# Two-layer transformer block: how VectorE finishes the mLSTM heads, and where it reads the causal mask

## What is computed

```
log_D = log_fg + ig                      (lower triangle, -inf above it)
D = exp(log_D - max_log_D)
C = (q @ k.T / sqrt(32)) * D
normalizer = max(|C.sum(-1)|, exp(-max_log_D))
h = (C / (normalizer + EPS)) @ v
hn = (h - h.mean(-1)) * rsqrt(h.var(-1) + EPS) * ln_scale        (over the 32 channels of a head)
x = x + hn
```

## Time and profile before

| | us |
|---|---|
| median of 3 runs | 1285.64 |
| lowest, highest | 1282.01, 1287.48 |
| the profiled execution, its own time | 1286.82 |
| span of its trace | 1285.0 |
| mean granted TensorE clock | 0.927 of full |
| PE busy | 1093.1 |
| DVE busy | 854.9 |
| ACT busy | 523.9 |
| POOL busy | 417.1 |

### The profile page before, as it was taken

How to read it: one execution, slowest core, us unless ns; L and a number is a source line. 1 busy time by engine, 2 the same in 40 slices (tenths; PEclk the granted TensorE clock), 3 DMA queues, 4 the chain that set the end, 5 groups by cost and what they waited for, 6 DMA issues and landing times. The chain is left out here.

```text
span 1285.0 us, 21982 instructions
## 1 busy us (share of the span) xinstructions
PE 1093.1 (85%) x6180; PEld 826.6 (64%) x6198; DVE 854.9 (67%) x1561; ACT 523.9 (41%) x1092; POOL 417.1 (32%) x327
## 2 busy tenths in 40 slices
PE   6999799788887759887859996999999999999842
PEld 6989666434443428777847764777777777777630
DVE  3547449878875628888756895767677676766415
ACT  1332152366674258677524242433333333333210
POOL 0000001111110201666733001456566556655420
PEclk8999899999999788888768999999999999999975
DMA  7323500100000486534063312878789898777539
GB/s 276 135 98 155 204 25 1 17 1 0 0 1 1 154 287 224 199 145 181 1 248 145 71 56 82 238 182 231 187 235 233 203 234 224 200 191 176 81 63 378
DMA packets 100284, 185.19 MB, mean 144 GB/s; under 512 B 13737, under 2 KB 32425, under 8 KB 100240
## 3 DMA queue, kind: packets, MB, share of 16 engines
q1 hardware_dynamic: 79856, 141.33, 32.6%
q0 software_dynamic: 18080, 38.85, 15.6%
q10 hardware_dynamic: 2304, 4.46, 0.9%
HBM read 138.50 MB, written 50.86 MB: 147 GB/s over the span
## 5 line engine op out<-in xcount | busy, mean ns | idle before, releaser
L2235 POOL DMA_INDIRECT y_d<-tail,x_ox x80 | 169.0, 2112 | 135.6 <-ACT tail L2400 110.1
L1536 POOL DMA_INDIRECT x_g<-r_d,x_ix x82 | 87.2, 1063 | 138.6 <-issue 115.6
L2293 PE MATMUL x_h<-x_w_hi,x_t_hi 128*128 x320 | 128.1, 400 | 2.2 <-DVE x_t_lo L2416 2.2
L2294 PE MATMUL x_h<-x_w_lo,x_t_hi 128*128 x320 | 127.7, 399 | 0.0
L2295 PE MATMUL x_h<-x_w_hi,x_t_lo 128*128 x320 | 127.7, 399 | 0.0
L210 POOL TENSOR_TENSOR ln_rstd<-ln_ve,powers 128x2 f32<-128x2 f32 (+1 forms) x40 | 26.2, 655 | 265.5 <-DVE ln_ve L204 265.5
L2416 DVE TENSOR_TENSOR x_w_lo<-w,x_w_hi (+1 forms) x64 | 109.6, 1753 | 2.6 <-ACT x_w_hi L2374 2.6
L2365 ACT ACTIVATE x_gs<-x_h 128x256 f32<-128x256 f32 x80 | 30.7, 385 | 187.5 <-PE x_h L2295 172.4
L2416 DVE TENSOR_TENSOR x_t_lo<-x_xb,x_t_hi 128x512 fp32r<-128x512 f32 x80 | 55.3, 692 | 43.0 <-ACT x_t_hi L2360 42.8
L1268 ACT ACTIVATE h_d<-h_negm,h_g 128x256 f32<-128x256 f32 x128 | 63.7, 498 | 28.6 <-DVE h_negm L1440 26.8
L2312 PE MATMUL x_o<-x_w_hi,x_avt_hi 128*128 x160 | 72.0, 450 | 1.5 <-issue 1.1
(11 more groups left out here) (371 smaller groups left out, 2671.8 us busy)
## 6 DMA issues: line engine op xcount, KB each, us to landing
w<-in_L_ffn_w SPq DMA_DIRECT2D x32, 1024.0 KB, 8.6
h_negm<-negm_d SPq DMA_DIRECT2D x16, 1024.0 KB, 7.1
w<-in_L_ffn_w SPq DMA_DIRECT2D x32, 512.0 KB, 10.0
raw<-in_L_ffn_w SPq DMA_DIRECT2D x3, 2816.0 KB, 16.8
x_res<-in_x SPq DMA_DIRECT2D x8, 512.0 KB, 4.9
ctx_in<-in_ctx SPq DMA_DIRECT2D x8, 512.0 KB, 3.5
...
```

The source lines that it names most:

```text
L1536: nc.gpsimd.indirect_dma_start(out=xg[q][s][:], out_offset=None, in_=r_d, in_offset=bass.IndirectOffsetOnAxis(ap=ix[q][:, s:s + 1], axis=0 ...
L2235: nc.gpsimd.indirect_dma_start(out=y_d[s], out_offset=bass.IndirectOffsetOnAxis(ap=ox[q][:, s:s + 1], axis=0), in_=eo[q][s][:], in_offset= ...
L2293: nc.tensor.matmul(hbank[s][:], hi[:, k, :], w13p[0][:, at, k, :], start=k == 0, stop=False)
L2294: nc.tensor.matmul(hbank[s][:], hi[:, k, :], w13p[1][:, at, k, :], start=False, stop=False)
```

## The change

- The squares are taken of the raw rows, not of the divided ones: variance = nrm * nrm * (sum of raw squares) / 32 + EPS. The 1024-element division on DVE is gone; POOL multiplies the raw rows by ln_scale (one instruction of 1024 elements in place of two of 512), and the two factors var^-0.5 and nrm are multiplied on POOL (a new instruction on 32 columns) before they meet the rows. One buffer `hb` is left of two.
- DVE's finishing steps are three pieces: `norms_of` behind group 1 (3 instructions), `variance` behind group 2 (the sum alone), and the new `scale` behind group 3 (3 instructions on 32 columns, the last of which releases POOL's power).
- ACT's `square` moves from behind group 1 to behind group 0, and no longer waits for DVE.
- `later`, a copy of the causal mask, is made once in PSUM (DVE), and `mask` reads it there. The two banks of `tg` become one, and EPS is added where the floor is copied.
- `weigh` becomes two instructions of 768 elements, two heads each; `c_ready` and `qk_ps` count halves, and the scores of the first two heads of a group wait only for the first half of the weigh before.
- `soft_log(0)` on ACT stands one batch of gates earlier.
- The last batch's steps in `experts` are changed in the same way; `tail_divide` is gone, and its small steps stand in `tail_variance`.

The first product now waits for the raw rows alone; the power still waits for DVE, and one small product stands between the power and the big one. The diff, cut to its core (line numbers of the functions behind it shift by 2 to 15):

```diff
     hr = [sbuf(st, "h_raw", [P, CB, NH, W])[:], tail.raw]
-    hb = [sbuf(st, "h_b", [P, CB, NH, DH])[:], tail.h]
-    sq, nrm, var, rs = tail.sq, tail.nrm, tail.var, tail.rs
+    hb = tail.h
+    sq, nrm, nrm2, var, rs = tail.sq, tail.nrm, tail.nrm2, tail.var, tail.rs
 
 
     qk = psum(st, "h_qk", [P, HG, 512])
     pvb = [psum(st, f"h_pv{i}", [P, CB, HG + WIDE - 1, W]) for i in range(2)]
     gbank = [t[:].rearrange("p c h w -> p (c h w)")[0:2 * NH, 0:S] for t in pvb]
-    tg = [psum(st, f"d_tg{j}", [P, CB, BH]) for j in range(2)]
+    tg = psum(st, "d_tg", [P, 2, CB, BH])
+    later = psum(st, "h_later", [P, P])
 
     w_sum, a_step, g_step, xn_ready, xt_ps, xt_sb, g_ps, g_sb = (
...
@@ -1200,22 +1202,24 @@
 
         def finish(b, u):
 
-            h = hb[u]
-            flat = h.rearrange("p c h e -> p c (h e)")
-            pool.wait_ge(sq_ready, b + 1)
-            for c in range(CB):
-                steps.did(nc.gpsimd.tensor_tensor(flat[:, c], flat[:, c], lns[:], ALU.mult))
+            pool.wait_ge(h_sb, NG * b + NG)
+            nc.gpsimd.tensor_tensor(hb, hr[u][:, :, :, 0:DH],
+                                    lns[:].rearrange("p (h e) -> p h e", e=DH).unsqueeze(1).to_broadcast([P, CB, NH, DH]),
+                                    ALU.mult).then_inc(scaled, 1)
             pool.wait_ge(var_ready, OPEN + b + 1)
             nc.gpsimd.tensor_tensor(rs.rearrange("p c h -> p (c h)"), var.rearrange("p c h -> p (c h)"),
                                     powers[:, 0:1].to_broadcast([P, CB * NH]), ALU.pow).then_inc(rs_ready, 1)
             pool.wait_ge(rs_ready, OPEN + b + 1)
-            steps.settle()
-            steps.then(nc.gpsimd.tensor_tensor(h, h, rs.unsqueeze(3).to_broadcast([P, CB, NH, DH]), ALU.mult))
-            nc.gpsimd.tensor_tensor(x[:, ds(CB * b, CB), :], x[:, ds(CB * b, CB), :], flat, ALU.add).then_inc(x_added, 1)
-
-        for opened in (rs_ready, x_added):
+            nc.gpsimd.tensor_tensor(rs, rs, nrm, ALU.mult).then_inc(factor_ready, 1)
+            pool.wait_ge(factor_ready, OPEN + b + 1)
+            pool.wait_ge(scaled, OPEN + b + 1)
+            steps.then(nc.gpsimd.tensor_tensor(hb, hb, rs.unsqueeze(3).to_broadcast([P, CB, NH, DH]), ALU.mult))
+            rows = x[:, ds(CB * b, CB), :]
+            steps.then(nc.gpsimd.tensor_tensor(rows, rows, hb.rearrange("p c h e -> p c (h e)"), ALU.add))
+
+        for opened in (rs_ready, factor_ready, scaled):
             pool.sem_inc(opened, OPEN)
-        with steps.loop(0, B // 2 - 1, 6) as i:
+        with steps.loop(0, B // 2 - 1, 4) as i:
             for u in range(2):
                 finish(2 * i + u, u)
...
@@ -1273,13 +1277,14 @@
 
             if k == 0:
                 act.wait_ge(h_read, OPEN + b - 1)
+                act.wait_ge(scaled, OPEN + b - 1)
             act.wait_ge(pv_ps, NG * b + k + 1)
             nc.scalar.copy(hr[u][:, :, HG * k:HG * (k + 1), :], pvb[k % 2][:, :, 0:HG, :]).then_inc(h_sb, 1)
 
         def square(b, u):
-            act.wait_ge(h_read, OPEN + b + 1)
+            act.wait_ge(h_sb, NG * b + NG)
             act.wait_ge(var_ready, OPEN + b)
-            nc.scalar.activation(sq, hb[u], ACT.Square).then_inc(sq_ready, 1)
+            nc.scalar.activation(sq, hr[u][:, :, :, 0:DH], ACT.Square).then_inc(sq_ready, 1)
 
         def batch(b, m, u, first=False, final=False):
             for k in range(NG):
@@ -1296,7 +1301,7 @@
                     take(b, k - 1, u)
                 elif not first:
                     take(b - 1, NG - 1, 1 - u)
-                if k == 1 and not first:
+                if k == 0 and not first:
                     square(b - 1, 1 - u)
             if not final:
                 stage_v(b + 1, m + u, 1 - u)
...
@@ -1306,7 +1311,7 @@
         queries(0)
         for b in range(1, B):
             queries(b)
-            if b == B - 2:
+            if b == B - 3:
                 soft_log(0)
             gates(b - 1)
         gates(B - 1)
...
         def scores(b, k, u):
             n = NG * b + k
-            after(pe, c_ready, n)
             for j in range(HG):
+                if j % HH == 0:
+                    after(pe, c_ready, 2 * n - 1 + j // HH)
                 r = slice(DH * j, DH * (j + 1))
                 nc.tensor.matmul(qk[:, j, 0:S], kt[r, u, k, 0:P], qt[r, u, k, :], start=True, stop=True)
                 last = nc.tensor.matmul(qk[:, j, S:S + P], kt[r, u, k, P:S], qt[r, u, k, P:S], start=True, stop=True)
-            last.then_inc(qk_ps, 1)
+                if j % HH == HH - 1:
+                    last.then_inc(qk_ps, 1)
 
         def values(b, k, u):
             n = NG * b + k
-            pe.wait_ge(c_ready, n + 1)
+            pe.wait_ge(c_ready, 2 * n + 2)
             pe.wait_ge(v_staged, b + 1)
             after(pe, h_sb, n - 1)
             for j in range(HG):
...
@@ -1427,9 +1434,9 @@
             nc.vector.tensor_tensor(fl[r], cum[r], mx[r], ALU.add).then_inc(fl_in, 1)
 
         def gate_columns(n):
-            for j, dst in enumerate((g_t, floor_t)):
-                dve.wait_ge(t_ps, 2 * n + j + 1)
-                nc.vector.tensor_copy(dst[:, :, part(n)], tg[j][:, :, part(n)]).then_inc(t_sb, 1)
+            dve.wait_ge(t_ps, 2 * n + 2)
+            nc.vector.tensor_copy(g_t[:, :, part(n)], tg[:, 0, :, part(n)]).then_inc(t_sb, 1)
+            nc.vector.tensor_scalar(floor_t[:, :, part(n)], tg[:, 1, :, part(n)], M_EPS, None, ALU.add).then_inc(t_sb, 1)
 
         steps = Steps(dve, dve_step)
...
@@ -1438,34 +1445,39 @@
             heads = slice(HG * k, HG * (k + 1))
             dve.wait_ge(rows_ld[u][k // 2], 16 * m + 16)
             nc.vector.tensor_tensor(nm[:, u, heads, 0::2, :], nm[:, u, heads, 0:2, :],
-                                    future[:].unsqueeze(1).unsqueeze(1).to_broadcast([P, HG, 2, P]),
+                                    later[:].unsqueeze(1).unsqueeze(1).to_broadcast([P, HG, 2, P]),
                                     ALU.add).then_inc(masked, 1)
 
         def weigh(b, k):
             n = NG * b + k
             dve.wait_ge(d_ready, n + 1)
             after(dve, pv_ps, n - 1)
-            dve.wait_ge(qk_ps, n + 1)
-            nc.vector.scalar_tensor_tensor(cm[:, k % 2], qk[:, :, 0:3 * P], float(DH) ** -0.5,
-                                           dm[:, k % 2].rearrange("p j c n -> p j (c n)"),
-                                           ALU.mult, ALU.mult).then_inc(c_ready, 1)
-
-        def divide(b, u):
-
+            for f in range(2):
+                heads = slice(HH * f, HH * (f + 1))
+                dve.wait_ge(qk_ps, 2 * n + f + 1)
+                nc.vector.scalar_tensor_tensor(cm[:, k % 2, heads], qk[:, heads, 0:3 * P], float(DH) ** -0.5,
+                                               dm[:, k % 2, heads].rearrange("p j c n -> p j (c n)"),
+                                               ALU.mult, ALU.mult).then_inc(c_ready, 1)
+
+        def norms_of(b, u):
+
+            own = hr[u][:, :, :, DH]
             dve.wait_ge(h_sb, NG * b + NG)
-            steps.then(nc.vector.scalar_tensor_tensor(nrm, hr[u][:, :, :, DH], -1.0, hr[u][:, :, :, DH], ALU.mult, ALU.max))
-            steps.then(nc.vector.tensor_tensor(nrm, nrm, floor_t[:, :, ds(b * NH, NH)], ALU.max))
-            steps.then(nc.vector.tensor_scalar(nrm, nrm, M_EPS, None, ALU.add))
+            dve.wait_ge(factor_ready, OPEN + b)
+            nc.vector.scalar_tensor_tensor(nrm, own, -1.0, own, ALU.mult, ALU.max).then_inc(h_read, 1)
+            dve.wait_ge(h_read, OPEN + b + 1)
+            steps.then(nc.vector.scalar_tensor_tensor(nrm, nrm, M_EPS, floor_t[:, :, ds(b * NH, NH)], ALU.add, ALU.max))
             steps.then(nc.vector.reciprocal(nrm, nrm))
-            dve.wait_ge(x_added, OPEN + b - 1)
-            nc.vector.tensor_tensor(hb[u], hr[u][:, :, :, 0:DH], nrm.unsqueeze(3).to_broadcast([P, CB, NH, DH]),
-                                    ALU.mult).then_inc(h_read, 1)
 
         def variance(b):
             dve.wait_ge(sq_ready, b + 1)
             dve.wait_ge(rs_ready, OPEN + b)
-            steps.then(nc.vector.tensor_reduce(var, sq, AX.X, ALU.add))
-            nc.vector.tensor_scalar(var, var, 1.0 / DH, M_EPS, ALU.mult, ALU.add).then_inc(var_ready, 1)
+            steps.did(nc.vector.tensor_reduce(var, sq, AX.X, ALU.add))
+
+        def scale(b):
+            steps.then(nc.vector.tensor_tensor(nrm2, nrm, nrm, ALU.mult))
+            steps.then(nc.vector.scalar_tensor_tensor(var, var, 1.0 / DH, nrm2, ALU.mult, ALU.mult))
+            nc.vector.tensor_scalar(var, var, M_EPS, None, ALU.add).then_inc(var_ready, 1)
 
         def batch(b, m, u, first=False, final=False):
             for k in range(NG):
@@ -1474,10 +1486,12 @@
                     mask(m, k + 2, u)
                 elif not final:
                     mask(m + u, k + 2 - NG, 1 - u)
-                if k == 0 and not first:
-                    divide(b - 1, 1 - u)
+                if k == 1 and not first:
+                    norms_of(b - 1, 1 - u)
```

(47 more changed lines are left out.)

8 lines of the change are left out of this document (4 added, 4 removed).

## The result

The changed kernel takes **1278.21 us** (median of 6 runs, 1276.29 to 1281.95) against 1285.41 for the kernel before beside it: ratio **0.9942 [0.9927, 0.9957]**. So it is faster, by 7 us, where 26 were forecast. The profiled execution took 1277.94 us, with a span of 1276.1.

What follows compares the result with a forecast made beforehand. DVE and its wait for POOL were taken to bound a batch at 16.4 us. Five such batches, the last and POOL's final list ended at 620.8 against 646.6; plus 0.5, a 26.3 us gain: 1260 us, range 1252 to 1279.

Steps and rivals of the forecast that it cites:

- z: Moment in each batch when `scale` ends and releases POOL; the forecast put the next one at z + 16.4 us.
- rival B: `norms_of` on DVE loses the port race to POOL twice; a batch takes about 20.0 us, 1278 us in all; 18%.
- the forecast's branch: In `norms_of`, only the second step is held, by POOL's big product until z + 8.2; batch 16.4 us; 55%.
- rival A: PE is the bound: `norms_of`'s second step slips through, a batch takes 14.9 us, 1253 us in all; 12%.
- POOL's list for the last batch: POOL's work after the last release, z7 = 610.1, was to end 10.7 us later, at 620.8.
- A hole of 1.50 us left the clock full: PE's waits: from scores of 0.74 us after such a hole, none was priced at the lower clock.
- 10 us or less in place of 33.7: Sign to look for: PE's idle before scores falls from 33.7 us to 10 us or less.
- D: The mask on DVE still waits for POOL though it reads PSUM: +1 to 2 us in all, 1262 us; 7%.
- C: Several short PE waits a batch keep its clock low; 1326 us if all four groups are slow; 8%.
- the part of B that I had priced at +3.1: In rival B, PE's hole exceeds 2 us and a slow group follows: +3.1 us a batch, partly in slack.

Runs made afterwards that it cites:

- e11: e2 with the floor read from SBUF, leaving one `norms_of` step with two SBUF inputs: 1259.06 us, ratio 0.9778 to the kernel before.
- e2: Changed kernel with `norms_of` in place but at most one SBUF input per step, ACT taking the sums' absolute value: 1253.48 us, 0.9752 of the kernel before.
- e3: Changed kernel with `weigh` as one instruction again, counts by groups: 1274.21 us, ratio 0.9903 to the kernel before.
- e8: e2 with `weigh` whole, in one instruction: 1253.82 us, ratio 0.9737 to the kernel before.
- e5: Changed kernel with `mask` reading the causal mask from SBUF again: 1287.47 us, ratio 1.0004 to the kernel before.
- e6: The kernel before with one part of the change alone, `mask` reading a copy in PSUM: 1280.25 us, ratio 0.9943 to the kernel before.
- e4: Changed kernel with the first `soft_log` back at its old place: 1277.96 us, ratio 0.9936 to the kernel before.
- e1: Changed kernel with `norms_of` moved from behind group 1 to behind group 3, just ahead of `scale`: 1257.61 us, ratio 0.9781 to the kernel before.
- e9: e2 with the mask read from SBUF again: 1262.59 us, ratio 0.9811 to the kernel before.

## Why the prediction was wrong

The side was right (faster, at 0.82), and the time was inside the range, 1252 to 1279, by less than one microsecond. The size was wrong by 18 us.

**The step that failed** is "Its first step runs at z + 6.15; its second finds POOL in the big product, and stands until z + 8.2; with the reciprocal it is done at z + 8.8." DVE kept the timetable: the step was issued at 521.61, z + 6.1. POOL did not: I had its product at z + 6.3, and it came at z + 5.9. In the other two batches with two holds DVE lost by 0.05 and 0.04 us (558.98 against POOL's 558.93, 596.50 against 596.46). DVE's time was right in part by luck: I had its masks done at z + 5.75 and the rest a wait for `factor_ready`; in fact `factor_ready` came at z + 5.83, and the masks lasted until z + 5.9 to 6.1, with 0.1 us behind `scale` and short gaps between the groups that my sum left out. The small product measured 0.25 us where I took 0.4, and the gaps ahead of it and behind it 0.08 us each where I took 0.16 and 0.2. I had named this as rival B, put the margin at tenths of a microsecond, and then gave it 18% because the timetable, which proved 0.4 us off, said so. Between a forecast and its rival that lie closer than the error of the sum, even odds were due. e11 shows the forecast's branch, e2 rival A's (14.87; forecast 14.9), after B's.

**The second half of the step**: B took DVE's next step at 0.14 us behind the held one, and so inside POOL's gap of 0.20, a toss-up. It came 0.51 us behind it in the batch shown and 0.27 in the other two, and POOL's add, 0.13 to 0.14 us behind it, was first in all three.

The miss, term by term, in the profiled executions (1277.94 - 1260.5 = 17.4 us):

- five batches of 18.73 instead of 16.4: +11.7; the last, z6 to z7, 16.31 instead of 14.2: +2.1. In all **13.8**: the second hold in every other batch, the slow group behind it, and DVE's wait for that group. e2, with no hold, shows none of them, and e11, with one, is 0.26 us a batch under the forecast.
- batch 0: batch 1 began at 500.96 instead of 498.4, +2.6; 0.6 of it is there already at the first weigh (480.50 against 479.90 before). In batch 0 PE idles for 10 to 13 us and starts at 0.50; the clock was up again by 489 us in the kernel before, by 493 in the changed one and by 487 in e3. From first weigh to fifth e3 took 18.3 us, e2 and e8 some 20 with halves and whole. Why the clock rose later is not settled.
- batch 1: -0.5. POOL's list for the last batch: 10.24 us instead of 10.7, -0.5.
- the rest of the program, from POOL's last add to the end of the span: 640.4 us against 638.4 before, +2.1. Among the other profiled executions it is 636.3 (e2) to 643.7 (e5) with the same code, so I don't put it down to the change.

That B's 1278 is the measured time to a microsecond is luck: B had 20.0 us a batch and got 18.7, and batch 0 and the rest of the program, which it did not have, made up for it.

**Two readings of rows that were wrong**, though neither moved the sum: e11, which is the forecast's batch, shows no such hole, and the idle time in batch 0 is no term of it. "A hole of 1.50 us left the clock full" looked at the scores alone; the clock fell right behind them. The first two rows are of the kernel before, the last two of e6 behind a hole of 1.51 us (windows, columns as in the earlier trace rows):

```profile
506.03:507.50 1.47, 1.47 (x21) 1.35 (x22) 1.40 (x2) 0.36 (x1) 1.45 (x1) 1.00 1.02 415
508.00:511.00 3.00, 3.00 (x16) 3.00 (x15) 3.00 (x3) 2.02 (x6) 1.48 (x2) 0.50 0.50 205
...
506.68:508.20 1.52, 1.52 (x21) 1.40 (x22) 1.44 (x2) 0.42 (x1) 1.50 (x2) 1.00 1.05 421
508.20:511.00 2.80, 2.80 (x33) 2.70 (x35) 2.80 (x3) 2.80 (x10) 1.02 (x1) 1.00 0.74 304
```

PE's idle before scores, in turn, could not come to "10 us or less in place of 33.7", since 12.80 of the 33.7 lie in batch 0, which the change does not touch.

**Right**: the masks at 1.21 us; DVE's hold ending with POOL's instruction; POOL ending behind ACT's last take, 6.7 us (628.98 to 635.68) against 7.4 forecast; two halves of weigh 1.74 us, start to start; DVE's own sum, since from the end of `norms_of` to the next z it is 7.77 us (526.30 to 534.07) against 4.11 + 3.53 = 7.64. `soft_log` at nothing (e4).

**The other rivals.** A did not happen, as POOL was first. D did not: no mask was held. C as told, several short waits a batch, was not put to the test: PE had one hole of 2.3 to 2.5 us every second batch and one of 0.2 to 0.6 between them, and in e1 and e2 none at all before scores between the first z and the sixth. e9 had one of 0.5 us in each of five batches, and its granted clock from the first z to the sixth was 1.00. So no run here shows the swing of which the Trainium skill (TensorE: Matmul & The Clock Gate, "A second HAM failure mode: psum-queue depth-cycling") tells. What came was the slow group behind a hole, the part of B that I had priced at +3.1: its group cost DVE 1.59 + 0.79 us of waiting in the next batch.

**Not seen beforehand**: that the mask alone gives the change's ratio. I gave the mask 1.5 of the 4.4 us that a batch was to lose, and the rest to DVE's shorter list and to steps that no longer meet POOL. Measured, a batch lost 2.3 us, 1.0 of it by the mask (e5, e6) and 1.3 by all the rest, and the later release, batch 0 and the rest of the program took back what the rest gave. The shorter list is worth 15.0 - 14.35 = 0.65 us a batch by the forecast's sums, a third of one held step.
